# The tail of a decoder layer: a last product in three fp32r terms, a reciprocal as exp(-ln) with a Newton step, norm constants on GpSimd, and the norm pieces of the last attention rounds behind the factors

## The reference

```python
# WKV, per channel, over time
y = (A * p + E * vt) / (A * q + E)
# feed-forward: 64 arrows of rank 16, the 4 longest chosen per token
vecs = jnp.einsum('arh,bsh->bsar', A, x)
arrows = jnp.linalg.norm(vecs, axis=-1)
_, idx = jax.lax.top_k(arrows, TOPK)
routes = jax.nn.one_hot(idx, arrows.shape[-1], dtype=x.dtype).sum(-2) / TOPK
v = jnp.einsum('bsa,bsar->bsr', routes, vecs)
delta = jnp.einsum('bsa,ajr,bsr->bsj', routes, B, v)
base = jnp.einsum('bsh,jh->bsj', x, W) + bias
return base + delta
# after each part
m = jnp.mean(x, axis=axis, keepdims=True)
v = jnp.var(x, axis=axis, keepdims=True)
return (x - m) / jnp.sqrt(v + eps)
```

## Time and profile before

| | us |
|---|---|
| median of 3 runs | 3062.6 |
| lowest and highest | 3057.56, 3067.12 |
| the profiled execution, own time | 3062.48 |
| its span | 3060.7 |
| PE busy in the span | 2884.2 (94%) |
| DVE busy | 2663.7 (87%) |
| ACT busy | 1941.1 (63%) |
| POOL busy | 613.6 (20%) |

### The profile page before, as it was taken

One profiled execution on the slowest core, in us unless ns is written; L12 is line 12 of the kernel. 1 busy time (PEld: TensorE's weight loads), 2 busy tenths in 40 slices (PEclk: granted clock), 3 DMA queues, 4 the chain that ended last, 5 costly groups with the idle time before them and its releaser, 6 DMA issues. The chain is left out here.

```text
span 3060.7 us, 78831 instructions
## 1 busy us (share of the span) xinstructions
PE 2884.2 (94%) x28584; PEld 2369.2 (77%) x28584; DVE 2663.7 (87%) x6377; ACT 1941.1 (63%) x6331; POOL 613.6 (20%) x902
## 2 busy tenths in 40 slices
PE   6899999999999999999999999999999999749998
PEld 4788887888888888888888888888888888636665
DVE  4698988999898889888989898988889898879995
ACT  3576666676767676666766666666676766544442
POOL 1121212121212112121212111212121221132221
PEclk9899999999999999999999999999999999869999
DMA  6434433343334343434334333334344433120000
GB/s 255 136 97 110 122 105 117 103 122 108 106 100 124 106 123 101 122 95 118 90 108 123 109 116 108 115 109 121 86 120 110 123 102 101 32 93 25 28 19 18
DMA packets 498474, 315.75 MB, mean 103 GB/s; under 512 B 314150, under 2 KB 453542, under 8 KB 480424
## 3 DMA queue, kind: packets, MB, share of 16 engines
q1 hardware_dynamic: 498088, 310.70, 34.6%
HBM read 243.07 MB, written 50.73 MB: 96 GB/s over the span
## 5 line engine op out<-in xcount | busy, mean ns | idle before, releaser
L1088 DVE SCALAR_TENSOR_TENSOR conv<-xb,convw,conv 128x512 f32<-128x512 f32 x768 | 592.0, 774 | 81.0 <-ACT conv L797 66.2
L580 PE MATMUL bank<-x_hi,w_hi 128*128 128x512 f32 x1024 | 429.7, 420 | 9.7 <-PEq L266 6.3
L580 PE MATMUL bank<-x_hi,w_lo 128*128 128x512 f32 x1024 | 403.2, 394 | 0.0
L580 PE MATMUL bank<-x_lo,w_hi 128*128 128x512 f32 x1024 | 400.5, 391 | 0.0
L791 ACT ACTIVATE xb<-bank 128x512 f32<-128x512 f32 x256 | 161.3, 630 | 302.7 <-PE bank L580 278.1
L592 PE MATMUL bank<-w_hi,x_hi 128*128 128x256 f32 x1024 | 304.4, 297 | 3.8 <-ACT conv L797 3.7
L592 PE MATMUL bank<-w_hi,x_lo 128*128 128x256 f32 x1024 | 290.4, 284 | 1.0 <-issue 1.0
L592 PE MATMUL bank<-w_lo,x_hi 128*128 128x256 f32 x1024 | 290.5, 284 | 0.0
L1171 POOL TENSOR_TENSOR small<-small,half 128x4 f32<-128x4 f32 x64 | 64.5, 1007 | 1034.2 <-DVE small L915 1034.2
L1199 POOL COPY halo<-xb 128x12 f32<-128x12 f32 x256 | 90.2, 352 | 839.3 <-ACT xb L791 839.0
L580 PEld LDWEIGHTS bank<-x_hi,w_hi 128*128 128x128 f32 x1024 | 194.1, 190 | 47.1 <-issue 9.0
(11 more groups left out here) (276 smaller groups left out, 7643.6 us busy)
## 6 DMA issues: line engine op xcount, KB each, us to landing
x_hi<-x_hi_scratch SPq DMA_DIRECT2D x63, 1024.0 KB, 5.0
x_lo<-x_lo_scratch SPq DMA_DIRECT2D x63, 1024.0 KB, 8.2
E<-decay_scratch SPq DMA_DIRECT2D x64, 512.0 KB, 5.2
M_scratch<-M SPq DMA_DIRECT2D x128, 256.0 KB, 2.4
w_raw<-in_w_proj SPq DMA_DIRECT2D x64, 384.0 KB, 8.5
U<-Ut SPq DMA_DIRECT2D x256, 64.0 KB, 2.0
w_raw<-in_w_out SPq DMA_DIRECT2D x32, 256.0 KB, 3.0
Mt<-M_scratch SPq DMA_DIRECT2D x256, 32.0 KB, 1.9
```

Source lines behind the costliest of these rows:

```text
L580: mm = pe.matmul(banks[j % 2][:].rearrange("p (b t) -> p b t", b=B), lhsT=t[f"w_{p}"][:, k, j, :], rhs=t[f"x_{q}"][:, k], start=i == 0, st ...
L1088: dve.scalar_tensor_tensor(out=y3, in0=xb[:, :, i:i + C], scalar=t["convw"][:, j, i:i + 1], in1=y3, op0=ALU.mult, op1=ALU.add).then_inc(on ...
```

## The change

Five things change.

1. The last product becomes three fp32r terms. B is loaded in four pieces into the buffers that held A's raw pieces (once A's low parts exist), and is split in round -2 into `B_hi` by ACT and `B_lo` by POOL, eight blocks of 128x512 each. ACT now writes the high part of zT, and a new DVE step `turn_z` writes the low part from the same PSUM bank. PE's next transposes into that bank and the product wait for the low part.
2. The reciprocal leaves DVE. A new ACT step `guess` takes Ln and then Exp of minus that; DVE's new `refine` makes one Newton step of two instructions, and stands in front of `quotient`, which becomes a three-operand instruction. The bounds of the exponents narrow from 60 and -80 to 44 and -44.
3. The two constants of each tail norm are made by POOL in `factor`, not by DVE.
4. In attention round 62 the statistics of norm 1 for chunk 1 move behind `x_part(r+1,0)`; in round 63 `factors` comes ahead of the statistics of chunk 2, on DVE and on POOL.
5. ACT loads the function table with Ln and Exp once at the tail's start. p, q, num and y have one buffer where they had two, the raw parts of W lie in other buffers, and the table `times` has two slots in place of four.

```diff
             if solve:
                 base(r + 1)
-            if r == NS - 2:
-                norm1(1)
             if state:
                 output(r)
                 update(r)
...
+            if state:
+                factors(r)
             if r == NS - 1:
                 norm1(2)
-            if state:
-                factors(r)
             if ahead:
                 taps(r + 2, 1, range(early, TAPS - 1))
                 taps(r + 2, 2)
             if solve:
                 turn_T(r + 1, 0)
                 x_part(r + 1, 0)
+            if r == NS - 2:
+                norm1(1)
...
             if r == NS - 1:
                 norm1(1)
+            if state:
+                factors(r)
+            if r == NS - 1:
                 norm1(2)
-            if state:
-                factors(r)
...
         sp.dma_start(t["iota"][:], a["iota"]).then_inc(on["d_tables"], 16)
-        sp.dma_start(t["ffn_B"][:], a["ffn_B"].rearrange("(k p) n -> p k n", p=128)).then_inc(on["d_tables"], 16)
+        for j in B_order:
+            sp.wait_ge(on["AB_lo"], j + 1)
+            sp.dma_start(B_raw(j), a["ffn_B"][j * 256:(j + 1) * 256].rearrange("(k p) n -> p k n", p=128)).then_inc(on[f"d_A{j}"], 16)
...
             pe.wait_ge(on["zz"], i + 1)
             if 2 * i + h:
-                pe.wait_ge(on["zT"], 2 * i + h)
+                pe.wait_ge(on["zT_lo"], 2 * i + h)
...
         def product(i):
-            pe.wait_ge(on["zT"], 2 * i + 2)
-            pe.wait_ge(on["d_tables"], 32)
+            pe.wait_ge(on["zT_lo"], 2 * i + 2)
+            pe.wait_ge(on["AB_lo"], KT + 8)
             for k in range(8):
-                mm = pe.matmul(joined(i)[:], lhsT=t["zT"][:, k, :], rhs=t["ffn_B"][:, k, :], start=False, stop=k == 7)
+                for p, q in PAIRS:
+                    mm = pe.matmul(joined(i)[:], lhsT=t[f"zT_{p}"][:, k, :], rhs=t[f"B_{q}"][:, k, :], start=False,
+                                   stop=(k, p, q) == (7, *PAIRS[-1]))
             mm.then_inc(on["product"], 1)
...
+        def split_B(k):
+            act.wait_ge(on[f"d_A{k // 2}"], 32)
+            act.activation(t["B_hi"][:, k], B_raw(k // 2)[:, k % 2], ACT.Copy).then_inc(on["AB_hi"], 1)
...
+        def guess(i):
+            act.wait_ge(on["den"], i + 1)
+            if i:
+                act.wait_ge(on["rden"], 2 * i)
+            act.activation(t["guess"][:], e(i)[:, :, own], ACT.Ln).then_inc(on["guess"], 1)
+            act.wait_ge(on["guess"], 2 * i + 1)
+            act.activation(t["guess"][:], t["guess"][:], ACT.Exp, scale=-1.0).then_inc(on["guess"], 1)
...
             act.wait_ge(on["arrows"], 2 * i + h + 1)
             if i >= 2:
                 act.wait_ge(on["zT_in"], 2 * (i - 2) + 2)
+            else:
+                act.wait_ge(on["AB_lo"], KT + 4 * i + 4)
...
+        act.preload_act_table_set("natural_log_exp_and_others")
         act.wait_ge(on["cols"], 9)
...
             if 0 <= r + 1 < NT:
                 squares(r + 1, 0)
+            if r + 3 < NT:
+                guess(r + 3)
             if r + 4 < NT:
                 weights(r + 4)
...
+                for k in B_blocks:
+                    split_B(k)
             if 0 <= r + 1 < NT:
                 squares(r + 1, 1)
...
             dve.bn_aggr(st[:, 0:2], st[:, 2:8]).then_inc(on[sem], 1)
-            dve.wait_ge(on[sem], 4 * i + 2)
-            dve.tensor_scalar(st[:, 8:9], st[:, 1:2], EPS_LN, None, ALU.add).then_inc(on[sem], 1)
-            dve.tensor_scalar(st[:, 10:11], st[:, 0:1], -1.0, None, ALU.mult).then_inc(on[sem], 1)
...
-        def reciprocal(i):
-            dve.wait_ge(on["den"], i + 1)
-            dve.reciprocal(e(i)[:, :, own], e(i)[:, :, own]).then_inc(on["rden"], 1)
+        def refine(i):
+            den, guess = e(i)[:, :, own], t["guess"][:]
+            dve.wait_ge(on["guess"], 2 * i + 2)
+            dve.tensor_tensor(den, den, guess, ALU.mult).then_inc(on["rden"], 1)
+            dve.wait_ge(on["rden"], 2 * i + 1)
+            dve.scalar_tensor_tensor(out=den, in0=den, scalar=-2.0, in1=guess, op0=ALU.add, op1=ALU.mult).then_inc(on["rden"], 1)
...
+        def turn_z(i, h):
+            span = slice(4 * h, 4 * h + 4)
+            dve.wait_ge(on["zT"], 2 * i + h + 1)
+            if i:
+                dve.wait_ge(on["product"], i)
+            dve.scalar_tensor_tensor(out=t["zT_lo"][:, span].rearrange("p k s -> p (k s)"), in0=banks[5][:], scalar=1.0 / TOPK ** 2,
+                                     in1=t["zT_hi"][:, span].rearrange("p k s -> p (k s)").bitcast(F32), op0=ALU.mult,
+                                     op1=ALU.subtract).then_inc(on["zT_lo"], 1)
...
+            if r >= 0:
+                turn_z(r, 0)
             if 0 <= r + 2 < NT:
                 norm2(r + 2)
...
-            if r + 3 < NT:
-                reciprocal(r + 3)
+            if r >= 0:
+                turn_z(r, 1)
             if 0 <= r + 2 < NT:
                 turn_x(r + 2)
             if 0 <= r + 1 < NT:
                 choose(r + 1)
                 spread(r + 1)
             if r + 3 < NT:
+                refine(r + 3)
                 quotient(r + 3)
...
+            pool.tensor_scalar(st[:, 8:9], st[:, 1:2], EPS_LN, None, ALU.add).then_inc(on[rstd], 1)
+            pool.tensor_scalar(st[:, 10:11], st[:, 0:1], -1.0, None, ALU.mult).then_inc(on[rstd], 1)
+            pool.wait_ge(on[rstd], 4 * i + 1)
             pool.tensor_tensor(st[:, 9:10], st[:, 8:9], mhalf, ALU.pow).then_inc(on[rstd], 1)
...
+            if r == -2:
+                for n, k in enumerate(B_blocks):
+                    split_B(n, k)
```

121 lines of the change are left out of this document (64 added, 57 removed).

## The result

The changed kernel takes **3114.6 us** (median of 4 runs, 3112.1 to 3121.1), the kernel before 3061.3 beside it: ratio 1.0187, 95% interval 1.0169 to 1.0205, so slower by nearly 2%. (All ratios here come from runs side by side; the quotient of the two medians is 1.0174, inside the interval.) The profiled execution took 3115.1 us with a span of 3113.2; that of before took 3062.5, so the difference to explain is +52.6, where +36.5 was forecast, and 3114.6 lies 1.6 above the upper end of the range, 3113.

A forecast was written before the change was run, and what follows sets the result against it. PE was taken to bound a tail round, DVE under a microsecond behind, with ACT's chain covering the reciprocal. Terms -4.9 + 4.6 + 1.65 + 35.4 + 2.6 - 2.9 + 0 = +36.5 on 3062.5 gave 3099 us, range 3078 to 3113.

The forecast's parts named there:

- ACT's norm at T+6: Tail round, T being DVE's third norm start: POOL's constants wait beside DVE's scans, so ACT's norm moves from T+4.78 to T+6.0.
- Rival A: Tail rounds: the stall doesn't form, the engines' own work sets a round of some 18.2 us; 3042 us, chance 0.07.
- rival C: Tail rounds: each of POOL's four small instructions sits behind a DVE instruction, ACT at T+8, +5 a round; 3123, chance 0.06.
- rival B: Tail rounds: POOL isn't last, its constants cost almost nothing, round 20.7 us, +1.6; total 3082, chance 0.12.
- The steady round: Rounds 0 to 11: 22.16 us for 19.14, +3.0 each, less 0.2 in rounds 9 to 11, together +35.4.
- T+6.8: Late bound for ACT's norm in a tail round, POOL's product behind the second scan or later: round 22.96 us, +3.8.
- In rounds 0 to 3 one more norm lies on DVE, before and after: Tail rounds 0 to 3: DVE has one more norm in both kernels; no extra time was put in the sum.
- Rival D: PE's waits drop the clock to the 1.2 GHz level for whole rounds, PE needing 35 us each; 3250, chance 0.02.
- Tail start: POOL's eight B blocks ahead of tile 1's norm delay the first choice by +2.6 to +7.5 us; taken as +4.6.
- Rounds 12 to 15: Last tail rounds: round 12 +2.6 us, rounds 13 and 14 together -2.9 with PE still the bound, round 15 zero.
- Attention: Rounds 62 and 63: moved statistics -2.9 and earlier factors -2.0, together -4.9 us; other end -2.5, zero not excluded.
- T+5.4: Early bound for ACT's norm in a tail round, with POOL's new constants at their low bound: round 21.56 us, +2.4.

The follow-up runs named there:

- e2: The changed kernel with the two constants of each tail norm back on VectorE: 3102.6 us, ratio 1.0143 to the kernel before.
- e6: The changed kernel with DVE's reciprocal back in its old place, without Ln, Exp and Newton step: 3077.8 us, ratio 1.0056 to the kernel before.
- e7: The changed kernel with Newton step and quotient ahead of DVE's second low part, ACT's exponentials and carries behind the second squares: 3082.0 us, ratio 1.0066.
- e3: The changed kernel with ScalarE's norm 1 moved one round later, behind the first zT half: 3114.1 us, ratio 1.0176 to the kernel before.
- e10: The changed kernel with eight unused PE matmuls in each of rounds 1 to 13 and ScalarE's norm 1 one round later: 3108.2 us, ratio 1.0157.
- e9: The changed kernel with eight unused matmuls filling PE's waits in each of rounds 1 to 13: 3115.5 us, ratio 1.0179 to the kernel before.
- e5: The changed kernel with the last product in plain float32 and no low parts of z and B: 3099.6 us, ratio 1.0123 to the kernel before.
- e4: The kernel before with only the change's moves in attention rounds 62 and 63: 3056.4 us, ratio 0.9984 to the kernel before.

## Why the prediction was right in kind and short in size

- **Sign and mechanism: right.** "ACT's norm at T+6", a wait on DVE in front of the second low part, PE waiting for z, a round of 22.16: measured T+6.66, 4.54 us, 1.37 us, 22.52. Rival A (the stall doesn't form) and rival C (ScalarE at T+8) fall with these rows, rival B (GpSimd isn't last) with the rounds that e2 shortened; e6 and e7 show that the stall is what costs.
- **The steady round, +3.0 forecast, +3.4 measured** (+2.8 and +3.2 where no carries are copied). The step "I take T+6.0" was 0.66 low: the first constant too fell beside the context product (0.69), the second beside the first scan (0.98), and the power beside the second (1.52, ending 0.4 behind that scan). T+6.8 was the stated bound. The part behind the choice was 8.69, not 8.9. That is 0.4 more than forecast in an undisturbed round; over the twelve intervals, with what else they take beyond norm 1 and the clock, it comes to 4.1 us of the miss.
- **"In rounds 0 to 3 one more norm lies on DVE, before and after": the step that failed.** It looked at DVE's copy of norm 1 and not at ScalarE's, which waits for GpSimd and stands ahead of the first half of z. In before nobody waited for that half until later; the change's own first low part of z does. The term was put at nothing and was 8.2 us in four intervals, shown by e3 and again by e10 against e9: the largest single part of the miss.
- **The clock.** Rival D had it fall for whole rounds or not at all, and the sum had nothing for it. It fell for parts of rounds, about 5.0 us in all by e9: 2.0 in the first twelve intervals, 1.5 in round 13 and 1.5 in the last product.
- **Tail start, +4.6 forecast, +7.9 measured**, just over its bound of 7.5. The step sized GpSimd's queue and let DVE's work beside it keep its time; from the first low part of W to the residual sum that work took 10.5 us instead of 4.3. That sum comes 5.6 later behind the start than in before. From it to ScalarE's norm it is 5.93 for 3.63; e5, which has the constants and no B parts, has 5.16, so 1.5 of these 2.3 are the constants' and 0.8 the end of the B queue's.
- **Rounds 12 to 15, +2.6, -2.9 and 0 forecast: right but for the clock.** From one third norm on DVE to the next (us):

| round | before | changed | e9 |
|---|---|---|---|
| 12 | 17.64 | 20.67 | 20.70 |
| 13 | 17.64 | 17.76 | 16.20 |
| 14 | 16.75 | 15.37 | 15.37 |
| 15, to the end of the span | 15.96 | 17.37 | 15.84 |

  "PE remains the bound" holds: where the clock doesn't fall, round 13 is 1.44 shorter and round 14 1.38, near the forecast's 1.46 each. Round 13 is 16.20 too in e2 and e6, which have no fillers, and 17.59 in e5, which has the plain product. Round 12 took 3.0 more, not 2.6, and round 15 is as long as before but for the clock. The clock's 1.5 lies in each of the rounds 13 and 15. The stretch behind the last choice shows 0 in the table above because the 1.4 that round 14 saves and the 1.5 of the clock cancel in it.
- **One row that moved.** The interval of 23.35 us is 0.8 longer than the later 22.5: of this 0.6 is the instruction below, of which before has two in its second interval and none here, and 0.2 is the clock's (23.12 in e9). It was moved, not added.

```profile
2882.37 0.67 DVE L1561 SCALAR_TENSOR_TENSOR times<-tpos,eye 4x512 fp32r<-4x512 f32 x1
```
- **Attention, -4.9 forecast: right** (e4, within its wide interval). In the changed kernel's trace the moves give 2.9, of which 0.5 is lost again before the next round's output, and 2.4; another 4.8 lie ahead of both places, where the code is the same. That these 4.8 lie on this side is luck: without them this execution would have taken 3120. Two rows of it, of VectorE, answer to the earlier trace rows: the statistics of chunk 1 now late in the round, and the factors at once behind ScalarE's sums.

```profile
2650.24 2.46 DVE L1102 BATCH_NORM_STATS2 ln<-acc 128x6 f32<-128x512 f32 x4
...
2675.22 0.17 DVE L1065 TENSOR_TENSOR f<-ss,small 128x8 f32<-128x8 f32 x1 [1.34 <-ACT De L752]
```

The tail's miss of 20.7 us is so 3.3 at the start, 8.2 for norm 1, 5.0 for the clock, and 4.1 for T+6.0 and what else is longer in the twelve intervals; the attention's 4.6 beyond its forecast took part of it back. The range took its ends from T and the tail's start alone; the attention's other end, -2.5, which the prediction names, was not in it. Its lower end, 3084, doesn't follow either: T+5.4 and a first choice at +2.6 give about 3090. What stays open is why PE's waits bring the clock down in one round and not in another where they are longer.
